# Four buffers of expert rows in the combining stage, and a partition's eight rows of a sequence placed together

## The reference

```
x = x + attention(layernorm(x))       # 16 heads of 64, causal, latent keys and values of 32
x = x + ffn(layernorm(x))             # mixture of experts
x = x + ssm(layernorm(x))             # chunked state space layer with a convolution ahead of it
x = x + ffn(layernorm(x))             # the same mixture of experts again

def ffn(x):
    scores = softmax(x @ Wr)                       # 8 experts
    w, idx = top_k(scores, 2);  w = w / sum(w)     # two gates for each token
    y[e] = (silu(x @ Wg[e]) * (x @ Wu[e])) @ Wd[e] # 256 hidden features
    return sum_k w[k] * y[idx[k]] + (silu(x @ Sg) * (x @ Su)) @ Sd
```

## Time and profile before

| | us |
|---|---|
| median of 3 runs | 3225.33 |
| lowest, highest | 3221.89, 3227.55 |
| span of the profiled execution | 3058.8 |
| the profiled execution's own time | not given by the page |
| TensorE busy in the span | 2564.5 (84%) |
| VectorE busy | 2019.8 (66%) |
| ScalarE busy | 1803.4 (59%) |
| GpSimd busy | 853.6 (28%) |
| first combining stage, first load's issue to VectorE's last instruction in it | 1675.0 to 1737.2 |
| second combining stage and the stores, to the end | 2990.9 to 3058.8 |

### The profile page before, as it was taken

The page is one execution under the profiler, slowest core; times in us unless marked ns, Lnnn a source line. Parts: engine busy times, 40 slices in busy tenths (PEclk is TensorE's granted clock), DMA queues, the critical chain, the costliest instruction groups (busy, mean ns, idle before and its releaser), DMA issues.

```text
span 3058.8 us, 77303 instructions
## 1 busy us (share of the span) xinstructions
PE 2564.5 (84%) x26192; PEld 2090.3 (68%) x26193; DVE 2019.8 (66%) x5025; ACT 1803.4 (59%) x4422; POOL 853.6 (28%) x1042
## 2 busy tenths in 40 slices
PE   3899898989898998897997189999999987988990
PEld 2777777777777777776886166666766765776880
DVE  2677676767666776786665656666676666875664
ACT  2777777777777777563554155555556554654550
POOL 0000000000000000575566233424233224774660
PEclk9999999999999999776999598998999986768995
DMA  5221111112111210111322300000000000112225
GB/s 147 49 49 44 44 43 44 43 46 51 44 43 44 51 47 20 53 45 54 82 81 75 96 2 2 2 2 2 2 2 2 2 2 22 45 54 72 82 78 168
DMA packets 139323, 140.27 MB, mean 46 GB/s; under 512 B 30540, under 2 KB 105425, under 8 KB 138864
## 3 DMA queue, kind: packets, MB, share of 16 engines
q1 hardware_dynamic: 122096, 101.67, 13.2%
q0 software_dynamic: 16896, 34.12, 3.3%
HBM read 45.85 MB, written 40.54 MB: 28 GB/s over the span
## 4 chain that ended last, share of the span: by engine, by line
PE 55%; DVE 16%; issue 9%; ACT 9%; SPq 5%; DMA 4%; DVEq 1%; POOL 1%; ACTq 0%; POOLq 0%
PE psum L457 5%; PE psum L426 5%; PE psum L492 4%; SPq L412 3%; DVE state L1717 3%; PE psum L1514 3%; ACT probs L446 3%; PE psum L1137 3%; PE psum L1111 2%; DVE neg_max L435 2%; PE psum L1112 2%; PE psum L1562 2%; PE psum L1113 2%; DMA y<-y_tok 2%; PE psum L543 2%
## 5 line engine op out<-in xcount | busy, mean ns | idle before, releaser
L446 ACT ACTIVATE probs<-psum,neg_max 128x512 f32<-128x512 f32 (+3 forms) x1024 | 539.5, 538 | 244.7 <-DVE neg_max L435 242.6
L435 DVE TENSOR_REDUCE neg_max<-psum 128x1 f32<-128x512 f32 (+3 forms) x1024 | 457.3, 483 | 54.8 <-PE psum L427 25.8
L426 PE MATMUL psum<-ls,qs 96*128 96x512 f32 (+3 forms) x1024 | 383.6, 400 | 115.1 <-ACT probs L446 103.5
L457 PE MATMUL psum<-ident,probs 128*128 128x128 f32 x2560 | 431.4, 284 | 2.8 <-ACT probs L446 0.8
L324 POOL TENSOR_TENSOR rstd<-var_eps,half_neg 128x4 f32<-128x4 f32 x32 | 40.5, 1267 | 1115.3 <-DVE var_eps L320 1115.3
L426 PEld LDWEIGHTS psum<-ls,qs 96*128 96x128 f32 x1024 | 199.9, 195 | 219.2 <-ACT probs L446 164.3
L476 DVE COPY probs_t<-psum 128x512 f32<-128x512 f32 (+1 forms) x384 | 230.3, 600 | 147.5 <-PE psum L457 140.5
L1250 POOL DMA_INDIRECT y_tok<-yb,xb x272 | 267.3, 983 | 207.7 <-issue 116.9
L457 PEld LDWEIGHTS psum<-ident,probs 128*128 128x128 f32 x2560 | 275.9, 145 | 25.8 <-ACT probs_t L472 9.7
L914 POOL DMA_INDIRECT x_slot<-pay,pos_i x256 | 255.9, 1000 | 92.4 <-issue 77.2
L427 PE MATMUL psum<-causal_r,ident_r 128*128 128x128 f32 x1024 | 236.8, 244 | 0.0
(11 more groups left out here) (320 smaller groups left out, 6638.8 us busy)
## 6 DMA issues: line engine op xcount, KB each, us to landing
qs<-q_h SPq DMA_DIRECT2D x512, 64.0 KB, 2.0
xb<-x_slot SPq DMA_DIRECT2D x272, 66.0 KB, 1.8
qs<-q_l SPq DMA_DIRECT2D x256, 64.0 KB, 2.0
y<-y_tok SPq DMA_DIRECT2D x32, 512.0 KB, 3.8
y_tok<-yb,xb POOLq DMA_INDIRECT x272
x_sb<-in_x SPq DMA_DIRECT2D x16, 256.0 KB, 5.5
x_slot<-pay,pos_i POOLq DMA_INDIRECT x256, 2.3
out<-x_sb SPq DMA_DIRECT2D x16, 256.0 KB, 3.0
```

The source lines that it names most:

```text
L426: pe.matmul(o[:, at:at + n], q, ls[par][0:3 * LD, 0:n], start=(at == 0), stop=False, skip_group_check=True)
L435: last = dve.tensor_reduce(neg_max[:, par, h, qt:qt + 1], bank[u % 3][:, at:at + (qt + 1) * P], AX.X, ALU.max, negate=True)
L446: last = act.activation(probs[:, u % 3, c], bank[u % 3][:, c], ACT.Exp, bias=neg_max[:, par, h, qt:qt + 1], accum_out=row_sum[:, par, h, q ...
L457: last = pe.transpose(bank[3 + u % 2][:, c:c + P], probs[:, u % 3, c:c + P], ident[:, :])
```

## The change

The combining stage gets four buffers `y2` and not two. SP's load of sequence b waits for sequence b - 4, four sequences are written out on SP and VectorE, and a loop of three trips does four sequences each. The result of token t * 128 + p of sequence b goes to row b * 1024 + p * 8 + t * 2 + k of `y_tok`, so that the eight rows that partition p needs of a sequence lie one behind the other, and a load reads one piece of 4096 bytes for each partition. Two semaphores of the buffers are added; to make room, GpSimd's two counters `pay_ready` and `y_ready` become one (`go_pool`), and `c_zero` is dropped in favour of a second count on `c_made`. All of it:

```diff
+Y2_RING = 4
...
-        y2 = [sb(f"y2_{i}", [P, QT, TOPK, D]) for i in range(2)]
+        y2 = [sb(f"y2_{i}", [P, QT, TOPK, D]) for i in range(Y2_RING)]
...
-            pool.sem_inc(z["pay_ready"], 1)
+            pool.sem_inc(z["go_pool"], 1)
...
-                    pool.sem_inc(z["y_ready"], 1)
+                    pool.sem_inc(z["go_pool"], 1)
...
             def load(b, par):
-                if not (isinstance(b, int) and b < 2):
-                    sp.wait_ge(z["mixed"], f * SEQS + b - 1)
+                if not (isinstance(b, int) and b < Y2_RING):
+                    sp.wait_ge(z["mixed"], f * SEQS + b + 1 - Y2_RING)
                 sp.dma_start(y2[par][:, :, :, :], y_tok[f][bass.ds(b * L * TOPK, L * TOPK), :].rearrange(
-                    "(t p k) d -> p t k d", p=P, k=TOPK)).then_inc(z[f"y2_in{par}"], 16)
-
-            for b in range(2):
+                    "(p t k) d -> p t k d", p=P, k=TOPK)).then_inc(z[f"y2_in{par}"], 16)
+
+            for b in range(Y2_RING):
                 load(b, b)
-            with sp.Fori(1, PAIRS) as i:
-                load(2 * i, 0)
-                load(2 * i + 1, 1)
+            with sp.Fori(1, SEQS // Y2_RING) as i:
+                for j in range(Y2_RING):
+                    load(Y2_RING * i + j, j)
...
             def mix(b, par, use):
-                dve.wait_ge(z[f"y2_in{par}"], 16 * (f * PAIRS + use + 1))
+                dve.wait_ge(z[f"y2_in{par}"], 16 * (f * (SEQS // Y2_RING) + use + 1))
...
-            for b in range(2):
+            for b in range(Y2_RING):
                 mix(b, b, 0)
-            with dve.Fori(1, PAIRS) as i:
-                mix(2 * i, 0, i)
-                mix(2 * i + 1, 1, i)
+            with dve.Fori(1, SEQS // Y2_RING) as i:
+                for j in range(Y2_RING):
+                    mix(Y2_RING * i + j, j, i)
...
-            pool.iota(idall[:, :, :], pattern=[[P * TOPK, SEQS * QT], [1, TOPK]], base=0, channel_multiplier=TOPK)
+            pool.iota(idall[:, :, :].rearrange("p (b t) k -> p b t k", t=QT),
+                      pattern=[[L * TOPK, SEQS], [TOPK, QT], [1, TOPK]], base=0, channel_multiplier=QT * TOPK)
...
-            pool.memset(half_neg[:, :], -0.5).then_inc(s["c_zero"], 1)
-            pool.wait_ge(s["c_zero"], 1)
+            pool.memset(half_neg[:, :], -0.5).then_inc(s["c_made"], 1)
+            pool.wait_ge(s["c_made"], 1)
...
-            pe.wait_ge(s["c_made"], 1)
+            pe.wait_ge(s["c_made"], 2)
...
-            dve.wait_ge(s["c_made"], 1)
+            dve.wait_ge(s["c_made"], 2)
```

More of the change, by code:

```diff
@@ L282, in program @@
         s = {n: sem(n) for n in (
-            "x0_loaded x_loaded w_loaded c_zero c_made c_round w_hi wfold_mm wfold_hi wfold_done "
+            "x0_loaded x_loaded w_loaded c_made c_round w_hi wfold_mm wfold_hi wfold_done "
             "ln_var ln_eps ln_rstd ln_xn ln_t ln_hi ln_lo xt_free x_done "
@@ L293, in program @@
             "pos_sum pos_done gate_mm up_mm silu_done hid_done hid_hi hid_lo down_mm acc_done "
-            "pay_ready y_ready run_done t_step t_done tab_out pads_out "
+            "go_pool run_done t_step t_done tab_out pads_out "
             "xt_mm xt_hi xt_lo gu_mm gu_silu gu_mul ht_mm ht_hi ht_lo dn_mm dn_half dn_add "
-            "y2_in0 y2_in1 mixed_a mixed").split()
+            "mixed_a mixed").split()
               + [f"xb_in{j}" for j in range(RING)] + [f"y_out{j}" for j in range(Y_RING)]
-              + [f"pay_out{j}" for j in range(PAY_RING)]}
+              + [f"pay_out{j}" for j in range(PAY_RING)] + [f"y2_in{j}" for j in range(Y2_RING)]}
         block = ctx.enter_context(nc.Block())
```

## The result

| | before | after |
|---|---|---|
| median of 13 runs each, us | 3227.55 | 3208.33 |
| lowest to highest, us | 3213.38 to 3250.31 | 3196.21 to 3221.20 |
| ratio to before, 95% interval | | 0.9936 (0.9915 to 0.9957) |
| span of the profiled execution, us | 3058.8 | 3211.7 |

The change makes the kernel 19 us faster by the medians, 14 to 27 by the interval; 3206.9 was predicted. The spans of the two profiled executions can't be compared: 153 us lie between them, the other way round. The last part of the experiments shows where they lie. Inside the combining stages they can, and there the two chains of the prediction are gone.

A forecast was written before the change was run, and what follows sets the result against it. The prediction took alternating loads and VectorE work in the combining stages, and the last load's issue ahead of the queued stores, as the bound. -5.9 - 12.5 = -18.4 us from 3225.3 gave 3206.9, range 3200 to 3215.

The forecast's parts named there:

- the two chains of the prediction: Combining stages: load and work alternate on each of two buffers, 6.68 us per round, 3.34 a sequence against VectorE's 2.81.
- The second stage: Second combining stage: last load issued 37.2 us after the stage's first instead of 49.8, 12.5 us less.
- The first: First combining stage: VectorE's work ends at 1731.3 instead of 1737.20, 5.9 us less.
- The head of a trip: VectorE's loop in the combining stages: the way back costs 0.5 us a trip beyond 0.39; ends 0 and 2.4.
- rival (a): VectorE's combining loop: the way back costs 2.4 us, not 0.5; 9.5 us back, 3216.4; chance 0.14.
- The landing: First load of each combining stage: pieces of 4096 bytes gain 0; ends 0 and 0.5 us for each stage.
- GpSimd beside VectorE in the first stage: First combining stage: sequence 2 starts earlier but runs beside GpSimd's instructions, gaining 0.8 us; bounds nothing and 1.49.
- Slack at the end: Second combining stage: store 15 issued at 52.1, sequence 15 done at 48.8; store queue sets the end, 3.3 us to spare.
- rival c: Expert stage: scatters to rows 4096 bytes apart crowd; over 6.5 us slower from landings of 11.0 us; chance 0.02.
- rival b: Combining stages: four loads in flight get only 155 GB/s, 3.38 us a sequence, total 3218.3; chance 0.03.
- rival d: TensorE after the first combining stage: clock granted elsewhere, some 5 us either way; chance 0.04 of no change or worse.
- Passed on in full: After the first combining stage: its 5.9 us gain reaches the following work in full.

## Why the prediction was right, point by point

*The bound.* As read: the loads' waits went, and the pace became VectorE's 2.81 us. *The second stage:* 37.2 predicted for the last load, 36.7 measured; the end 12.5 us earlier predicted, 13.2 measured. *The first:* 5.9 predicted, 6.1 measured. *The sum:* 18.4 against 19.3 in the profiles, or 18.2 with the second profile of before. It is closer than its terms: in the first stage GpSimd took 0.7 us more than I gave it, against 0.5 less in the loop and a landing 0.4 earlier; in the second I had the landing 0.2 and the two heads 0.5 us too long. That 3206.9 lies 1.4 us from 3208.33 is luck besides, since the base, a median of three runs, lay 2.2 us below the median of thirteen.

*The head of a trip,* taken at 0.5 us, is 0.20 for the first and 0.34 to 0.37 for the others; rival (a) is out. The whole loop costs 5.2 us in the first stage, as the version written out shows (47.44 for 52.67): by the rows 2.8 for its twelve gaps (0.38 for 0.15), 1.4 inside its sequences (2.43 us for 2.31) and 0.9 at the heads.

*The landing,* taken at no gain, gained 0.24 us for the first load of the second stage (3.82 in the earlier trace rows, 3.58 after): between the two ends of the term. Single landings vary by more. From that load's issue to VectorE's first instruction it is 3.79 to 3.86 us in the four profiles with the rows where they were, and 3.45 to 3.87 in the eight with the rows moved. By the rule of the Trainium skill, "DMA: Bandwidth & Descriptors" (Specifications), it would have been nothing; this case's medians say 0.2 us, and the measurement decides. With four buffers it hardly matters.

*GpSimd beside VectorE in the first stage.* I had sequences 0 to 3 end 17.3 us after VectorE's start, and they took 18.0 (1763.55 to 1781.54): the first two lost 0.4 more because the landing came 0.4 earlier against GpSimd's 3.8 us, so that VectorE stood longer beside it and the shorter landing gained nothing in this stage; the next two took 9.97 us, 5.2 above what they take without it. In the rows

```profile
1762.77 3.81 POOL L2045 TENSOR_TENSOR wx_tap<-wx_tap,wx_st 128x2048 f32<-128x2048 f32 x1
1771.25 6.09 POOL L2066 TENSOR_TENSOR wx_l<-wx_tap,wx_h 128x512 fp32r<-128x512 f32 x4 [1.94 <-ACT wz_h L1931]
```

GpSimd works for 9.9 us, and beside the second VectorE got one instruction done in about 1.6 us where it does one in 0.29. The Trainium skill, "SBUF — State Buffer" (SBUF: two separate sides), says that the two engines lock one pair of ports, for a whole instruction, where VectorE reads two operands from SBUF and GpSimd reads there too. The trace agrees. So 18.0 less the 9.7 that four sequences take alone, 8 us, are lost in the first stage; before it was 7 (2.7 in sequences 0 and 1, 4.2 in sequence 2). No run here moved it.

*Slack at the end.* Sequence 15 was mixed 48.1 us after the first load (48.8 predicted), and the last store issued after 51.5, so the queue of stores still set the end. *Scatters* (rival c): out; VectorE ahead of its sum waited for no scatter, the 68 sums of an expert stage take 212 us in either kernel on the lower level and 263 and 265 on the upper, and the kernel with the rows alone wasn't slower. *Transfers* (rival b): out, by 356 GB/s. *The clock* (rival d): over the 790 us behind the first combining stage the granted clock was 0.93 and 0.92 in the two profiles of before, 0.91 and 0.93 in the two of after; no change can be seen, and none was needed. *Passed on in full:* from VectorE's last instruction in the first stage to the second's first load it is 1253.7 us before and 1252.8 after, both on the lower level, which fits; but the same work took 1248.1 to 1264.8 us in the other profiles of that level, so the profiles don't show it to a few us, and the medians do only within their interval.

*What was wrong in the text.* I put 166.5 us around the span, from a median and a span that belong to two chips. The run that was profiled after took 3213.54 us with a span of 3211.7: 1.8 us lie around it. The sum held because the stages are alike on both.

*Rows of the kernel before that numbers of the prediction rest on and that no group ahead of it shows.* The page's chain by engine, and one load on the chain, from which the 6.68 us were taken:

```profile
PE 55%; DVE 16%; issue 9%; ACT 9%; SPq 5%; DMA 4%; DVEq 1%; POOL 1%; ACTq 0%; POOLq 0%
```

```profile
3034.02 3.80 DMA y<-y_tok
```

The timeline, with GpSimd's first instruction beside VectorE, the first sequence written out and the longest gap in the loop:

```profile
1677.66 3.81 POOL L2043 TENSOR_TENSOR wx_tap<-wx_tap,wx_st 128x2048 f32<-128x2048 f32 x1
...
2994.79 2.32 DVE L1288 SCALAR_TENSOR_TENSOR x_sb<-y,gates,x_sb 128x128 f32<-128x128 f32 x8 [8.81 <-DMA y<-y_tok]
...
3001.33 1.15 DVE L1288 SCALAR_TENSOR_TENSOR x_sb<-y,gates,x_sb 128x128 f32 x4 [1.76 <-DMA y<-y_tok]
```

VectorE's eight waits of 1.0 us in the expert loop, and the stretches of the DMA share 0.29, the granted clock 0.68 and the 288 GB/s:

```profile
DVE bh L1214 <- issue: 8.0, 8, 1.0
```

```profile
1550.00:1600.00 50.00, 47.64 (x317) 41.65 (x318) 30.19 (x63) 27.35 (x63) 30.65 (x32) 1.00 0.29 81
1750.00:1760.00 10.00, 10.00 (x33) 8.01 (x33) 1.54 (x4) 2.97 (x4) 6.68 (x15) 0.68 0.00 0
3048.00:3050.00 2.00, 0.00 (x0) 0.00 (x0) 0.00 (x0) 0.00 (x0) 0.00 (x0) 0.50 1.01 287
```

## What to carry to other kernels

Where an engine waits for loads though the DMAs are half idle, add the landing and the work of one buffer, divide by the number of buffers, and compare with the work alone: here 6.7 / 2 against 2.81, and from three buffers on (6.7 / 3) the work is the bound. Then look at what stands behind the loads in their queue: 5 of the 19 us came from stores that could start earlier before the work's end, which the profile's chain doesn't show. Once the work is the bound, what lies around it counts: written out, without the wait for its own last instruction and with the stores in another queue, it was worth as much again (20 us).

## What the runs showed of the hardware

One kernel has two levels of time, 3070 and 3230 us, on different chips here; 172 of the 177 us between two of its profiles lie in the routing and expert stages, where at the upper level several engines show waits without a releaser. A profile from one chip and times from another must not be set off against each other. Loads of 512 KB kept up at 512 KB every 2.23 us beside stores of 256 KB, with single landings of up to 6.3 us that cost nothing. And pieces of 4096 bytes instead of 1024 shortened the issue of a load from 373 to 333 ns and its landing by 0.2 us.
